# Attention and feed-forward on one core: other constants for the order of attention, and four moved steps at the two seams

## What is computed

```
q = (x @ Wq) in 32 heads;  k, v = halves of x @ Wkv          # one k, v for all heads
scores = q . k / sqrt(32) + slope_h * (pos_k - pos_q), masked to pos_k <= pos_q
h = layernorm(x + (softmax(scores) @ v) @ Wo)
r = the rank of (8, 16, 32, 64) with the highest h @ gate_w.T + gate_b
out = layernorm(h + h @ W.T + b + (h @ A[:r].T) @ B[:, :r].T)
```

## Time and profile before

| | |
|---|---|
| time, median of 3 | 3422.95 us (3421.85 to 3425.56) |
| the profiled execution | 3427.93 us, span 3426.2 us |
| granted TensorE clock, mean | 0.98 |
| busy: TensorE, its weight loads | 3293.6 us (96%), 2204.1 us (64%) |
| busy: VectorE, ScalarE, Pool | 2128.4 us (62%), 1702.6 us (50%), 1766.2 us (52%) |
| DMA | 215.34 MB, 63 GB/s in the mean |

### The profile page before, as it was taken

How to read it: one execution, slowest core, us unless ns; L and a number is a source line. 1 busy time by engine, 2 the same in 40 slices (tenths; PEclk the granted TensorE clock), 3 DMA queues, 4 the chain that set the end, 5 groups by cost and what they waited for, 6 DMA issues and landing times. The chain is left out here.

```text
span 3426.2 us, 54171 instructions
## 1 busy us (share of the span) xinstructions
PE 3293.6 (96%) x19553; PEld 2204.1 (64%) x19553; DVE 2128.4 (62%) x5166; ACT 1702.6 (50%) x3076; POOL 1766.2 (52%) x744
## 2 busy tenths in 40 slices
PE   5999999999999999999999999999987999999998
PEld 4666565555555555655555555555536999999997
DVE  5566677677777763566687767767714554445554
ACT  2546656666677766556656665667761110111100
POOL 3326657776787876235667757878891010000100
PEclk8999999999999999999999999999998999999999
DMA  3541221112110113332221111111103112121221
GB/s 88 143 118 57 75 79 47 50 50 61 34 56 26 50 40 96 93 94 77 69 75 57 50 44 35 47 29 41 66 28 99 56 59 70 55 73 55 64 64 44
DMA packets 214070, 215.34 MB, mean 63 GB/s; under 512 B 13876, under 2 KB 162356, under 8 KB 213784
## 3 DMA queue, kind: packets, MB, share of 16 engines
q1 hardware_dynamic: 213848, 212.46, 20.9%
HBM read 144.72 MB, written 67.17 MB: 62 GB/s over the span
## 5 line engine op out<-in xcount | busy, mean ns | idle before, releaser
L1077 ACT ACTIVATE prob<-ps_s,alibi 128x512 f32<-128x512 f32 (+3 forms) x2075 | 1226.8, 631 | 594.0 <-PE ps_s L1347 561.3
L1009 POOL TENSOR_TENSOR prob<-prob 128x2048 f32<-128x2048 f32 (+1 forms) x240 | 1046.3, 4370 | 446.9 <-PE ps_o L1354 412.3
L1194 DVE TENSOR_REDUCE mxp<-ps_a 128x1 f32<-128x512 f32 x1536 | 967.1, 680 | 311.4 <-PE ps_a L1333 307.2
L1333 PE MATMUL ps_a<-wol,qst 97*128 97x512 f32 (+3 forms) x2560 | 924.7, 384 | 35.4 <-DMA qst<-q_rows 16.8
L1347 PE MATMUL ps_s<-qst,kexp 97*128 97x512 f32 (+4 forms) x2075 | 800.0, 391 | 18.1 <-ACT prob L1077 12.5
L1299 PE MATMUL ps_m<-woh,wol 128*128 128x512 f32 x1704 | 643.2, 411 | 0.0
L1197 DVE CUSTOM_DVE_ANT_0 ps_a<-ps_a,maska 128x128 f32<-128x128 f32 (+3 forms) x1024 | 481.7, 513 | 251.9 <-PE ps_a L1333 232.0
L1333 PEld LDWEIGHTS ps_a<-wol,qst 97*128 97x128 f32 x2560 | 482.8, 191 | 206.3 <-DVE mxp L1197 70.3
L1347 PEld LDWEIGHTS ps_s<-qst,kexp 97*128 97x128 f32 (+1 forms) x2075 | 394.1, 191 | 300.0 <-ACT prob L1077 183.3
L1354 PE MATMUL ps_o<-prob,val 128*32 128x512 f32 (+3 forms) x5120 | 546.3, 539 | 9.3 <-ACT prob L1077 7.1
L1606 POOL TENSOR_TENSOR work<-work,bias_b 128x1024 f32<-128x1024 f32 x32 | 76.8, 2400 | 746.6 <-DVE work L1745 711.3
(11 more groups left out here) (130 smaller groups left out, 3283.8 us busy)
## 6 DMA issues: line engine op xcount, KB each, us to landing
qst<-q_rows SPq DMA_DIRECT2D x192, 256.0 KB, 3.9
work<-in_L_attn_hidden_states SPq DMA_DIRECT2D x64, 512.0 KB, 4.8
wq_raw<-in_L_attn_Wq SPq DMA_DIRECT2D x64, 512.0 KB, 4.1
q_rows<-wol SPq DMA_DIRECT2D x128, 256.0 KB, 2.1
att_scratch<-at_sb SPq DMA_DIRECT2D x64, 256.0 KB, 2.4
at_raw<-att_scratch SPq DMA_DIRECT2D x32, 512.0 KB, 5.3
out<-work SPq DMA_DIRECT2D x32, 512.0 KB, 3.1
work<-in_L_attn_Wo SPq DMA_DIRECT2D x8, 512.0 KB, 4.8
```

What stands on the lines that cost most here:

```text
L1009: nc.gpsimd.tensor_tensor(even[:, :, c1:], even[:, :, c1:], odd[:, :, c1:], ALU.add).then_inc(pair_done, 1)
L1077: nc.scalar.activation(prob[slot_of(step)][:, h, c0:], bank[:, c0:], ACT.Exp, bias=alibi_of(g, h, k - full_tiles(g))).then_inc(e_done, 1)
L1194: nc.vector.tensor_reduce(top, ps, AX.X, ALU.max).then_inc(a_done, 1)
L1333: last = nc.tensor.matmul(bank[:, 0:cols], qst[g % 3][0:KR, h, t * P:(t + 1) * P], kmax[0:KR, ring(sg):ring(sg) + cols], start=True, stop= ...
```

## The change

Ten constants of `Order` get other values. In the start, ScalarE makes the high parts of Wkv, ahead of its splits of x, and counts them in a semaphore of their own; VectorE makes the low parts; Pool waits for all four low parts before it fills `kexp`; and Pool makes the rows of query buffers 1 and 2 before it splits Wq for units 1 and 2. The low parts of Wo's pieces 4 to 7 are made by VectorE, with a second counter, and the planner books them there. In the feed-forward prologue the load of `at_raw` is issued first and the bias behind the W parts, EARLY is 2, and four of the eight turns of W stand between the products of the first tile, one behind each third piece of Wo.

```diff
--- before.py
+++ after.py
@@ -127,10 +127,10 @@
     S_BANKS, A_BANKS, M_BANK = (0, 1), (2, 3, 4), 5
     NEVER = 1.0e18
     FILL, DRAIN, LOAD, MODE_IN, MODE_OUT = 0.4567, 163, 104, 93, 90
-    SHORT, BATCH, MOST, PACE, MARGIN = 30, 3, 5, 30, 2000
-    LOOK, NARROW_SLACK = 100, 50
-    QE_GAP, X_GAP, K_GAP, WO_GAP = 300, 500, 300, 2000
-    BULK_GAP, W_GAP, QI_GAP, MASK = 100, 400, 100, 1100
+    SHORT, BATCH, MOST, PACE, MARGIN = 0, 3, 7, 10, 3000
+    LOOK, NARROW_SLACK = 200, 200
+    X_GAP, K_GAP, WO_GAP = 200, 600, 2000
+    BULK_GAP, W_GAP, QI_GAP, MASK = 100, 200, 100, 690
 
     def __init__(self, bank_counts):
         self.items = []
@@ -600,7 +600,7 @@
 
     def do_wo_low(self, at, c, half):
         self.put("WOL", c, half)
-        done = self.on_pool(at, 1285)
+        done = self.on_pool(at, 1285) if c < QT else self.on_dve(at, 1500, 1400)
         if half == 0:
             self.push(done + self.WO_GAP, self.do_wo_high, c, 1)
             return
@@ -786,6 +786,7 @@
         rows_done = sem("rows_done")
         dist_done = sem("dist_done")
         alibi_done = sem("alibi_done")
+        wkv_hi = sem("wkv_hi")
         wkv_done = sem("wkv_done")
         rows_out = sem("rows_out")
         wkv_in = sem("wkv_in")
@@ -820,7 +821,7 @@
         counters += [at_out] + later
         wo_in = [sem(f"wo_in{i}") for i in range(QT)]
         wo_hi = counter("wo_hi")
-        wo_lo = counter("wo_lo")
+        wo_lo = [counter(f"wo_lo{i}") for i in range(2)]
 
         s_full = counter("s_full")
         e_done = counter("e_done")
@@ -907,7 +908,7 @@
                 if c == 0:
                     sp.wait_ge(q_ps, START + UNITS)
                 if c >= QT:
-                    sp.wait_ge(wo_lo, START + 2 * (c - QT + 1))
+                    sp.wait_ge(wo_lo[c // QT - 1], START + 2 * (c % QT + 1))
                 if c < DC:
                     sp.dma_start(xs[:, at], wo_v[c]).then_inc(wo_in[at], 16)
                 else:
@@ -960,6 +961,7 @@
             nc.gpsimd.affine_select(out=maska[:, QB - P:], in_=maska[:, QB - P:], compare_op=ALU.is_ge, fill=MASKED, base=0,
                                     pattern=[[-1, P]], channel_multiplier=1).then_inc(pool_c, 1)
             pool.wait_ge(pool_c, 7)
+            pool.wait_ge(wkv_done, 4)
             mask_rows = kexp[3 * DH:P].bitcast(F32)
             nc.gpsimd.memset(mask_rows, BLOCKED).then_inc(key_rows, 1)
             pool.wait_ge(key_rows, 1)
@@ -971,7 +973,7 @@
 
             def make_query_rows(buf):
                 pool.wait_ge(key_rows, 3)
-                pool.wait_ge(wql_done, START + buf)
+                pool.wait_ge(wql_done, START + min(buf, 1))
                 below = qst[buf][3 * DH:P]
                 nc.gpsimd.memset(below.bitcast(F32), 1.0).then_inc(query_rows, 1)
                 pool.wait_ge(query_rows, 2 * buf + 1)
@@ -1015,19 +1017,20 @@
 
             def split_wo(c, half):
                 pool.wait_ge(wo_hi, START + 2 * c + half + 1)
-                if c == DC - 1:
-                    pool.wait_ge(q_out[half], START + 16 * UNITS)
                 cols = slice(half * QB, (half + 1) * QB)
                 nc.gpsimd.tensor_tensor(wol[:, c, cols], xs[:, c % QT, cols], woh[:, c, cols].bitcast(F32),
-                                        ALU.subtract).then_inc(wo_lo, 1)
-
-            for number in range(3):
-                make_query_rows(number)
-                split_wq(number)
+                                        ALU.subtract).then_inc(wo_lo[0], 1)
+
+            make_query_rows(0)
+            split_wq(0)
+            make_query_rows(1)
+            make_query_rows(2)
+            split_wq(1)
+            split_wq(2)
             for what, n, arg, bank, before, at in items:
                 if what == "WL":
                     split_wq(n)
-                if what == "WOL":
+                if what == "WOL" and n < QT:
                     split_wo(n, arg)
                 if what == "DIV":
                     divide(n)
@@ -1089,6 +1092,10 @@
                 cols = slice(half * QB, (half + 1) * QB)
                 nc.scalar.activation(woh[:, c, cols], xs[:, c % QT, cols], ACT.Copy).then_inc(wo_hi, 1)
 
+            act.wait_ge(wkv_in, 16)
+            for r in range(3):
+                nc.scalar.activation(wkvh[:, :, r * DH:(r + 1) * DH], wkv_raw[:, :, 0:DH], ACT.Copy).then_inc(wkv_hi, 1)
+            nc.scalar.activation(wkvh[:, :, 3 * DH:P], wkv_raw[:, :, DH:2 * DH], ACT.Copy).then_inc(wkv_hi, 1)
             for j in range(DC):
                 split_x(j, ps_a[a_bank(j)], j)
             for half in range(2):
@@ -1123,11 +1130,7 @@
             dve.wait_ge(slope_set, NH)
             for t in range(QT):
                 nc.vector.tensor_copy(slope4[:, :, t], slope[:]).then_inc(slope4_set, 1)
-            dve.wait_ge(wkv_in, 16)
-            for r in range(3):
-                nc.vector.tensor_copy(wkvh[:, :, r * DH:(r + 1) * DH], wkv_raw[:, :, 0:DH]).then_inc(wkv_done, 1)
-            nc.vector.tensor_copy(wkvh[:, :, 3 * DH:P], wkv_raw[:, :, DH:2 * DH]).then_inc(wkv_done, 1)
-            dve.wait_ge(wkv_done, 4)
+            dve.wait_ge(wkv_hi, 4)
             for r in range(3):
                 cols = slice(r * DH, (r + 1) * DH)
                 nc.vector.tensor_tensor(wkvl[:, :, cols], wkv_raw[:, :, 0:DH], wkvh[:, :, cols].bitcast(F32),
@@ -1196,6 +1199,14 @@
                     dve.sem_inc(went_on, 1)
                     nc.vector.tensor_tensor_reduce(ps, ps, maska[:, QB - cols:], 1.0, MASKED, ALU.add, ALU.max,
                                                    top).then_inc(a_done, 1)
+
+            def split_wo(c, half):
+                dve.wait_ge(wo_hi, START + 2 * c + half + 1)
+                if c == DC - 1:
+                    dve.wait_ge(q_out[half], START + 16 * UNITS)
+                cols = slice(half * QB, (half + 1) * QB)
+                nc.vector.tensor_tensor(wol[:, c, cols], xs[:, c % QT, cols], woh[:, c, cols].bitcast(F32),
+                                        ALU.subtract).then_inc(wo_lo[1], 1)
 
             def reduce_max(g, taken):
                 s = seg_of(g) % NSEG
@@ -1256,6 +1267,8 @@
                     take_v(n, banks[bank])
                 if what == "QL":
                     take_q(n)
+                if what == "WOL" and n >= QT:
+                    split_wo(n, arg)
                 if what == "R":
                     invert(n, arg)
 
@@ -1382,7 +1395,7 @@
                 if j > 2:
                     pe.wait_ge(a_done, START + j - 2)
                 turn_x(0, j, ps_a[a_bank(j)])
-            pe.wait_ge(wkv_done, 8)
+            pe.wait_ge(wkv_done, 4)
             for m in range(3 * DC):
                 project_kv(0, m, DC, ps_o)
             for m in range(3 * DC):
@@ -1505,7 +1518,7 @@
 
         NZ = 3
         RAW = DC + 2
-        EARLY = 3
+        EARLY = 2
         FIRST = DC
         raw_at = (1, 2, 3, 4, 5, 0, 1, 2, 0, 1)
         free_at = {6: 1, 7: 2, 8: 6, 9: 7}
@@ -1542,8 +1555,6 @@
 
         @block.sync
         def _(sp):
-            sp.dma_start(bias_b[:], bias.partition_broadcast(P)).then_inc(const_in, 16)
-            sp.dma_start(gate_bb[:], gate_b.partition_broadcast(P)).then_inc(const_in, 16)
             def load_raw(c):
                 if c in free_at:
                     sp.wait_ge(raw_lo, free_at[c])
@@ -1570,10 +1581,11 @@
             att_tiles = att.rearrange("(a g) t p q -> a t p g q", g=HG)
 
             def prologue():
-                load_raw(WORK - 1)
                 load_at(0, 0, 0)
-                for c in range(WORK, DC):
+                for c in range(WORK - 1, DC):
                     load_raw(c)
+                sp.dma_start(bias_b[:], bias.partition_broadcast(P)).then_inc(const_in, 16)
+                sp.dma_start(gate_bb[:], gate_b.partition_broadcast(P)).then_inc(const_in, 16)
                 sp.wait_ge(raw_lo, WORK - 1)
                 load_x(0)
                 sp.wait_ge(at_out, START + 16 * UNITS)
@@ -1792,7 +1804,7 @@
                         last = nc.tensor.transpose(dst, raw[:, k * P:(k + 1) * P], ident[:])
                 last.then_inc(raw_ps, 1)
 
-            def first_product(n, par):
+            def first_product(n, par, between=None):
                 pe.wait_ge(ath_done, START + n + 1)
                 pe.wait_ge(atl_done, START + n + 1)
                 pe.wait_ge(y_done, START + n)
@@ -1804,6 +1816,8 @@
                         nc.tensor.matmul(ps, ath[par][:, c], woh[:, c, cols], start=first, stop=False)
                         nc.tensor.matmul(ps, ath[par][:, c], wol[:, c, cols], start=False, stop=False)
                         last = nc.tensor.matmul(ps, atl[par][:, c], woh[:, c, cols], start=False, stop=end)
+                        if between is not None and c % 3 == 2:
+                            between()
                 last.then_inc(y_ps, 1)
 
             def second_product(n, p):
@@ -1846,9 +1860,10 @@
                 last.then_inc(z_ps, 1)
 
             def prologue():
```

(5 more changed lines are left out.)

## The result

The changed kernel takes **3362.82 us** (median of 4 runs, 3360.75 to 3367.63) against 3422.6 of the kernel before beside it (4 runs, 3421.85 to 3425.56): a ratio of 0.9826, 95% interval 0.9809 to 0.9843. Forecast was 3404, with 3382 to 3427 as the range. Its profiled execution took 3361.83 us, span 3360.1, so 66.1 less span than before. The medians are 59.8 apart: the profiled execution of the kernel before was 5.3 us above its median, so differences of traces against it come out some 5 us too large.

The account below looks back on a forecast made before the run. TensorE was taken to bound attention and the feed-forward loop, but not the seams. Start 3.4, Wo 3.4, prologue 5.2 and order 7 summed to 19 us off the median 3422.95, giving 3404 us, range 3382 to 3427.

Parts of the forecast that it names:

- The order: Attention: ten new planner constants change nearly every position; 7 us gained, bounds 45 gained and 30 lost.
- one run in ten merged: Attention: 41 runs of TensorE's 32-column form merged at 0.22 us each, 9, less 0.1 of standing each, 5 us.
- 2 for the masks: Attention: 2 us gained as MASK 1100 in the plan comes nearer to the measured 642 ns.
- 290 us of waits: Attention: of about 380 us beyond TensorE's floor, the 290 not put down to form changes; TensorE behind its banks.
- Rival 1: Attention: the order gives much more, 100 runs merged and 10 us of waits gone, 32 us: 3379; chance 0.15.
- Rival 4: Attention: slower by MOST at 7, tiles worked off in one go while ScalarE goes idle: 3443; chance 0.10.
- Rival 3: Attention: the order loses 5 to 19 us, 3416 to 3430, no change; chance 0.12.
- The start: Before the first scores: Wkv's high parts on ScalarE, Pool behind the low parts; cut 3.4 us, bounds 2.0 and 4.6.
- the wait that takes over: Start: Q of unit 0 waits for Pool's split of Wq, so 3.4 us are cut, not KV's 4.5.
- Wo on VectorE: Seam after attention: three low parts no longer stand on Pool behind the division; cut 3.4 us, bounds 2.4 and 4.0.
- "Nothing" for the five other pieces: End of attention: five more pieces of 1.28 us leave Pool's last 70 us; given nothing, bounds -2 and +1.
- The prologue: Feed-forward prologue: `at_raw` loaded first, four turns inside the first product; cut 5.2 us, bounds 2 and 7.4.

Follow-up runs that it names:

- pace30: The changed kernel with PACE 30 instead of 10: 3432.2 us, ratio 1.0028 to the kernel before.
- pace10_in_before: The kernel before with PACE 10 instead of 30 and nothing else: 3477.5 us, ratio 1.0169 to the kernel before.
- slack300: The changed kernel with NARROW_SLACK 300 instead of 200: 3392.3 us, ratio 0.992 to the kernel before.
- old_rules: The changed kernel with the ten old values of Order's constants, other steps kept: 3410.3 us, ratio 0.996 to the kernel before.
- wo_on_pool: The changed kernel, same list, with the low parts of Wo's pieces 4 to 7 on Pool again: 3373.9 us, ratio 0.9852 to the kernel before.
- mask690_in_before: The kernel before with MASK 690 instead of 1100 and nothing else: 3465.1 us, ratio 1.0132 to the kernel before.
- old_prologue: The changed kernel with the feed-forward prologue as before (bias first, EARLY 3, all turns ahead of the product): 3371.4 us, ratio 0.9841.
- old_start: The changed kernel with the start as before (Wkv's high parts on VectorE, Pool's set-up not waiting): 3370.9 us, ratio 0.9847.

## Why the prediction was wrong

**The order** is the step that failed: its term was 7 us, and it measured 51.7 in the traces and 41 to 47 by medians. I took "one run in ten merged" (41 x 0.22 = 9, less 4 of standing) and 2 for the masks, and gave nothing for the rest of the time between products, 290 us of waits. That many runs went (48, 10.6 us at 0.22). Beyond that the same products came closer together: of the 51.7 us, 31.1 were gained at full clock and 20.7 in the stretches at half clock. I had called the waits set by ScalarE and VectorE, "with 2 and 3 banks, which no constant adds to"; yet the time fell although the third bank took fewer scores, 409 instead of 485 (MARGIN says when it may be used). How many banks there are doesn't fix how the order spreads the scores over the time in which they come free. And my account had no term for the clock, though the row had 0.98 to show. Which single wait gave way stays open: neither the runs nor the rows of waits rank the orders.

Deeper lies the method: I priced the constants one by one and added. pace30 and pace10_in_before show that PACE 10 has no such price: within the ten it is worth 69 us, alone it costs 56, and MASK does the same with 36 and 43. The plan is a program that was at hand. Its clock alone, 2445.1 against 2404.9, would have given 40 us for the order, and 3371 for the whole. Rival 1 (the order gives 32 us) had the direction, with 0.15, and stood at 3379, 16 above the result; the range ended at 3382.

Rival 4 (MOST at 7) was void: with MOST at 5 the planner writes the same list, item for item. Rival 3, that the order loses, is what both single values did in the kernel before, and by more than I gave it. Of the rule of the Trainium skill, "TensorEngine Tiling (Array Packing)", Key Properties: the drain it speaks of is there, and fewer runs went with a gain here, but slack300 is the case against it as a guide: fewest runs, more time.

**The start**: forecast -3.4, measured -4.1 at the first exponential's scores (-3.4 to -4.6 in the four kernels with this start and list), each instant shown above within 0.8 us. Right, with the wait that takes over.

**Wo on VectorE**: 3.4 at the seam, measured 3.6 with the old list too (old_rules: 4.0 us at the seam); right. "Nothing" for the five other pieces, with a bound of 1, holds as far as seen for the old list, where Pool still stood for 1.88, 0.45 and 2.31 us in its last 70. For the new one it was the second mis-sized term: wo_on_pool shows about 5 us at the end of attention.

**The prologue**: forecast 5.2, measured 6.1, and 7.2 when undone; the bound was 7.4. Turns between products and the early load stand where it was said.

## What to carry to other kernels

Where an order comes out of a planner, run the planner and compare what it gives; its constants may have no prices that add, and one of them moved alone can cost as much as all of them bring. Don't expect of an order picked by the plan all that the plan promises: the one tried here gave 13 of 21 us. And before a moved piece of work is costed at nothing, look at whether the engine it leaves has any gap before the end.

## What the runs showed of the hardware

**VectorE and Pool in each other's way.** The eight low parts of Wo on VectorE, and Pool's additions, in the changed kernel (count, then ns as least, median, most):

```profile
L1208 DVE TENSOR_TENSOR wol<-work,woh x8: 933/1660/3907, 2467.7 to 2504.4; 128x512 fp32r<-128x512 f32 x8
```

```profile
L1011 POOL TENSOR_TENSOR prob<-prob x240: 3439/4584/5030, 244.1 to 2507.2; 128x2048 f32<-128x2048 f32 x96, 128x1536 f32<-128x1536 f32 x24
```

and the same eight with the old order (old_rules):

```profile
L1208 DVE TENSOR_TENSOR wol<-work,woh x8: 667/1007/4976, 2515.5 to 2552.0; 128x512 fp32r<-128x512 f32 x8
```

The same instruction takes 667 ns or 4976, where Pool takes 1284 for it at each time. The longest is about as long as one addition of Pool (4.58). It agrees with the Trainium skill, "SBUF — State Buffer", Who interferes with whom, on instructions that both read SBUF. VectorE was idle there, but Pool was not, and it pays too: six of its additions beside these parts take 4.79 to 5.03 us in the changed kernel, 2.2 us more in all than at 4.57:

```profile
2479.26 10.01 POOL L1011 TENSOR_TENSOR prob<-prob 128x2048 f32<-128x2048 f32 x2
2489.35 4.88 POOL L1016 TENSOR_TENSOR prob<-prob 128x2048 f32<-128x2048 f32 x1
```

In wo_on_pool none of its last nine of this size is above 4.58. So the move takes 10.3 us of pieces off Pool (8 x 1.284) and gives 2.2 back.

**Time at half clock.** With the same products, half clock took 50.0 us in the changed kernel and 119.5 in pace10_in_before. Over the first ten lists of the table it grows roughly with the time beyond the lengths at full clock (correlation 0.87), but mask690_in_before has as much of that as pace10_in_before (368.9 and 369.0) and no more half clock than the kernel before (88.7). That waits bring the clock down is a reading, not shown.

**Equal programs** differ by some us in attention from one execution to the next: 2456.4, 2459.6, and 2460.9 and 2461.5 in old_prologue and old_start, whose lists are the same. At full clock their time beyond the lengths is 302.7, 302.1, 302.4 and 300.4; at half clock it is 27.5, 31.3, 32.3 and 34.9. So the scatter is in the stretches at half clock, and these orders are told apart best by what they lose at full clock.
